# Weighted and plain neighbour sums: rows stored in source order and gathered in destination order, one-hots and rows in fp32

## The reference, cut to what matters

```python
# layer 3 (weighted): row = src, col = dst, deg = number of edges that leave a node (at least 1)
norm = edge_weights / jnp.sqrt(deg[row] * deg[col])
out  = segment_sum(x[row] * norm[:, None], col, num_segments=N)
# layer 4 (plain): edges and self loops, deg of both
norm = deg_inv_sqrt[row] * deg_inv_sqrt[col]
out  = segment_sum(label_mat[row] * norm[:, None], col, num_segments=num_nodes)
```

## Time and profile before

| | us |
|---|---|
| median of 3 runs (19801.2 to 19824.42) | 19813.48 |
| span of the profiled execution, first to last instruction | 17009.2 |
| `spread1`, from 14870 to 15608 | 738 |
| `tally1`, from 15608 to 15910 | 302 |
| `spread0`, from 16005 to 16606 | 601 |
| `tally2`, from 16606 to 16916 | 310 |
| `edge_keys`, up to its last gather | 2271 |

### The profile page before, as it was taken

How to read it: one execution, slowest core, us unless ns; L and a number is a source line. 1 busy time by engine, 2 the same in 40 slices (tenths; PEclk the granted TensorE clock), 3 DMA queues, 4 the chain that set the end, 5 groups by cost and what they waited for, 6 DMA issues and landing times. The chain is left out here.

```text
span 17009.2 us, 405783 instructions
## 1 busy us (share of the span) xinstructions
PE 9949.2 (58%) x119882; PEld 7747.5 (46%) x119882; DVE 11124.4 (65%) x27289; ACT 5234.6 (31%) x15775; POOL 9202.6 (54%) x10645
## 2 busy tenths in 40 slices
PE   2000047777777647974896599569926666433454
PEld 1000024444444237864785488458824444333324
DVE  6830046777776767985897599759954555466757
ACT  0000012222222014651564266236613333221120
POOL 7777777777777104431442244124427777585270
PEclk9755555555555569987997899699958777756656
DMA  3833357677678437645663666276612222134445
GB/s 117 327 93 102 102 87 80 85 85 85 85 86 79 80 102 209 176 126 150 186 176 91 196 176 176 56 227 176 175 48 61 65 65 65 45 129 143 148 152 161
DMA packets 2548685, 2116.02 MB, mean 124 GB/s; under 512 B 418374, under 2 KB 2314590, under 8 KB 2541593
## 3 DMA queue, kind: packets, MB, share of 16 engines
q1 hardware_dynamic: 2225086, 1439.58, 31.2%
q0 software_dynamic: 309216, 539.46, 19.4%
q10 hardware_dynamic: 14216, 135.01, 2.3%
HBM read 1290.57 MB, written 726.03 MB: 119 GB/s over the span
## 5 line engine op out<-in xcount | busy, mean ns | idle before, releaser
L627 POOL DMA_INDIRECT attend_rows<-key_rows,attend_fetch_now x1824 | 1747.7, 958 | 2056.5 <-PE attend_seg L1670 1729.3
L1714 ACT ACTIVATE attend_hot<-attend_lane_hot,attend_share 128x128 f32<-128x128 fp8e4 x7296 | 2228.5, 388 | 1209.9 <-DVE attend_share L1737 976.5
L627 POOL DMA_INDIRECT edges_rows<-raw,edges_perm_now x1824 | 2007.5, 1101 | 629.1 <-issue 602.4
L627 POOL DMA_INDIRECT keys_rows<-table,keys_staged x1564 | 1658.6, 1060 | 471.0 <-issue 471.0
L1670 PE MATMUL attend_seg<-attend_rows,attend_hot 128*128 128x49 f32 x14592 | 1816.8, 278 | 122.9 <-ACT parts_layer L1718 85.7
L1670 PEld LDWEIGHTS attend_seg<-attend_rows,attend_hot 128*128 128x128 f32 x14592 | 1734.3, 195 | 207.1 <-issue 201.9
L627 POOL DMA_INDIRECT mlp_xin<-table,mlp_staged x1564 | 1511.3, 966 | 472.7 <-issue 469.3
L1044 PE MATMUL edges_ps_t<-ident,edges_attr 128*40 128x128 f32 x1824 | 425.4, 413 | 1861.6 <-ACT edges_attr L1099 1833.9
L633 POOL DMA_INDIRECT messages<-spread_out,spread_place_now x912 | 1027.9, 1127 | 385.9 <-issue 276.5
L1657 PE MATMUL attend_qx<-attend_table,attend_oht 128*128 128x90 bf16 x21888 | 1087.8, 207 | 124.8 <-DMA attend_oht<-src_hots 113.0
L1481 POOL COPY expand_table<-k 128x156 bf16 x912 | 289.3, 317 | 1602.4 <-issue 947.3
(11 more groups left out here) (517 smaller groups left out, 23761.4 us busy)
## 6 DMA issues: line engine op xcount, KB each, us to landing
key_rows<-expand_out SPq DMA_DIRECT2D x304, 624.0 KB
attend_ea<-edge_attrs SPq DMA_DIRECT2D x912, 160.0 KB
tally_rows<-messages SPq DMA_DIRECT2D x152, 864.0 KB, 4.8
attend_table<-q SPq DMA_DIRECT2D x1832, 67.5 KB
expand_oht<-dst_hots SPq DMA_DIRECT2D x304, 384.0 KB, 4.8
attend_oht<-src_hots SPq DMA_DIRECT2D x912, 128.0 KB
attend_lane_hot<-src_hots_by_edge SPq DMA_DIRECT2D x912, 128.0 KB
raw<-keys_rows ACTq DMA_DIRECT2D x46, 2176.0 KB
```

The lines of the kernel that those rows point to most:

```text
L627: return nc.gpsimd.indirect_dma_start(out=out, out_offset=None, in_=table, in_offset=bass.IndirectOffsetOnAxis(ap=index, axis=0))
L1714: ins = nc.scalar.activation(hot[p][:, u, c, :], lane_hot8[r][:, u, c, :], ACT.Copy, scale=share[p][:, u, c:c + 1])
```

## The change

`spread` now serves both layers. VectorE writes fp32 rows straight from PSUM to `out` (a product with the weights, or a copy), with no split, and GpSimd stores the chunk as it is, in source order, with one plain DMA of 576 KB to `k.rows_a` ("rows_by_source"). `tally` gathers in place of loading: six indirect DMAs of 128 rows of 768 bytes per chunk, from the places in `k.origin`, into a ring of four. The one-hots are fp32, and TensorE does 24 fp32 matmuls a chunk in place of 72 bf16 ones. The zeroing of `k.msg` is gone; one row of each partition of `k.rows_a` is zero, for granules that no source has. `k.origin` is the inverse of `k.place`, and is built in `edge_keys` after the sort, with the same steps as `k.place`.

```diff
@@ edge_keys, SyncE
-            with sp.Fori(0, ZEROS) as n:
-                sp.dma_start(k.msg.rearrange("(p u) w -> p (u w)", p=P)[:, bass.ds(n * ZW, ZW)], zeros[...]).then_inc(s_out, 16)
+            sp.dma_start(k.rows_a.rearrange("(p r) w -> p r w", p=P)[:, NS, :], zeros[:, 0:GR * F]).then_inc(s_out, 16)
@@ edge_keys, VectorE, behind the sort
+            for q in range(4):
+                dve.wait_ge(s_mm, 13 + q)
...
+                for half in (slice(0, P // 2), slice(P // 2, P)):
+                    ch.done(v.tensor_tensor(under, rows_of(level[0:UT, :], P // 2), bc(k.iota[0:UT, half], KB), ALU.is_le))
+                    ch.done(v.tensor_tensor(under, under, rows_of(jump[0:UT, :], P // 2), ALU.mult))
+                    ch.done(v.tensor_reduce(at[0:UT, q, half], under, AX, ALU.add))
...
+            ch.done(v.tensor_tensor(k.origin[:], k.origin[:], part, ALU.add))
@@ spread, GpSimd
-                for u in range(EX):
-                    scatter(nc, k.msg, place_now[:, r, u:u + 1], out[r][:, u, :], NS * P - 1).then_inc(s_scat[r], 16)
+                pool.wait_ge(s_ev, (n + 1) * EX)
+                pool.dma_start(k.rows_a.rearrange("(p r) w -> p r w", p=P)[:, bass.ds(n * EX, EX), :], out[r][:]).then_inc(s_kept[r], 16)
@@ spread, VectorE
-                split(v, ch, msg[:], [by3[r][:, :, j, :] for j in range(3)], rest[:])
+                    if weighted:
+                        ins = v.tensor_tensor(out[r][:, u, :]..., got..., bc(k.w_a[:, ...], F), ALU.mult)
+                    else:
+                        ins = v.tensor_copy(out[r][:, u, :], got)
@@ tally, GpSimd (new) and SyncE (gone)
-                sp.dma_start(rows[b][:], k.msg.rearrange("(u p) w -> p u w", p=P)[:, bass.ds(n * EX, EX), :]).then_inc(s_load[b], 16)
+                pool.wait_ge(s_now, n + 1)
+                after(pool, s_seg, n - RINGS + 1)
+                for u in range(EX):
+                    gather(nc, rows[r][:, u, :], k.rows_a, origin_now[:, r, u:u + 1]).then_inc(s_rows[r], 16)
@@ tally, TensorE and VectorE
-        hot = [ph.sb(f"hot{b}", [P, EX * GR, P], BF16) for b in two]
+        hot = [ph.sb(f"hot{b}", [P, EX * GR, P]) for b in two]
-                        for j in range(3):
-                            ins = nc.tensor.matmul(ps[b][...], hot[b][:, u * GR + c, :], rows[b][:, u, at:at + F], ...)
+                        ins = nc.tensor.matmul(ps[b][...], hot[b][:, u * GR + c, :], rows[r][:, u, c * F:(c + 1) * F], ...)
+                    listed(n + 2, (r + 2) % RINGS)      # VectorE: 6 places per lane for the gathers two chunks on
```

More of the change, by code:

```diff
@@ L64 @@
 EX = 6
[L65 to L68, removed]
 KDOT = F + 2
@@ L423, in _ @@
             ins.then_inc(s_perm, 1)
+            pe.wait_ge(s_inv, 1)
+            t.transpose(small[0:NT, 128:128 + NT], base[0][0:NT, 0:NT], k.ident[0:NT, 0:NT]).then_inc(s_mm, 1)
+            for q in range(4):
+                pe.wait_ge(s_inv, 2 + q)
+                t.matmul(small[0:UT, 256:256 + KB], ended[0:NT, q * UT:(q + 1) * UT], base[1][0:NT, :], start=True, stop=True)
+                t.matmul(small[0:UT, 320:320 + KB], ended[0:NT, q * UT:(q + 1) * UT], steps[0:NT, :], start=True, stop=True).then_inc(s_mm, 1)
+            pe.wait_ge(s_inv, 6)
+            for q in range(4):
+                ins = t.transpose(wide[:, q * UT:(q + 1) * UT], at[0:UT, q, :], k.ident[0:UT, 0:UT])
+            ins.then_inc(s_mm, 1)
         @block.vector
@@ L2337, in _, with spread @@
             v.tensor_copy(k.tail[:, 0:F], sums[1][:, C - 1, :]).then_inc(s_step, 1)
-def spread(nc, k):
+def spread(nc, k, weighted):
     CHN, RINGS = NS // EX, 4
     with ExitStack() as ctx:
-        ph = Phase(nc, ctx, "spread1")
-        two = range(2)
+        ph = Phase(nc, ctx, "spread1" if weighted else "spread0")
+        two, ring = range(2), range(RINGS)
         oht = [ph.sb(f"oht{b}", [P, EX, W // 2], BF16) for b in two]
@@ L2420, in _ @@
             v = nc.vector
-            ch = Chain(dve, s_step)
-            by3 = [out[r][:].rearrange("p u (c j f) -> p (u c) j f", c=GR, j=3) for r in ring]
             def step(n, r, t):
+                after(dve, s_kept[r], t * 16)
                 for u in range(EX):
                     dve.wait_ge(s_exp, n * EX + u + 1)
[L2427 to L2431, removed]
-                split(v, ch, msg[:], [by3[r][:, :, j, :] for j in range(3)], rest[:])
-                dve.sem_inc(s_msg, 1)
@@ L2435, in _ @@
[L2435 to L2438, removed]
[L2439 to L2446 removed]
+                    got = ps[u][:, 0:GR * F]
+                    if weighted:
+                        ins = v.tensor_tensor(out[r][:, u, :].rearrange("p (c f) -> p c f", f=F), got.rearrange("p (c f) -> p c f", f=F),
+                                              bc(k.w_a[:, bass.ds((n * EX + u) * GR, GR)], F), ALU.mult)
+                    else:
+                        ins = v.tensor_copy(out[r][:, u, :], got)
@@ L2467, in steps @@
                 step(r, r, 0)
-            with eng.Fori(1, CHN // RINGS) as t:
+            with eng.Fori(1, LOOPS - 1) as t:
                 for r in ring:
                     step(t * RINGS + r, r, t)
+            for r in ring:
+                step((LOOPS - 1) * RINGS + r, r, LOOPS - 1)
         block = ph.block()
@@ L2543, in tally @@
[L2543 to L2575 removed]
+                pe.wait_ge(s_rows[r], (t + 1) * (16 * EX))
```

175 lines of the change are left out of this document (57 added, 118 removed).

## The result

The changed kernel took 19916.59 us (median of 4, 19895.34 to 19974.88) against 19807.34 (median of 4, 19799.03 to 19824.42) of the kernel before: ratio 1.0059, interval 1.0041 to 1.0076, +109 us. Timed again later it was 1.0113 (1.0096 to 1.0129), +223 us. Forecast were +262 us and 20075. The direction was right, and 19916.59 lies inside the stated range, 7 us above its lower end; the size was off by more than half in the first timing and by 15% in the second.

A forecast was written before the change was run, and what follows sets the result against it. It took GpSimd's queue of scatters to bound both spreads, and VectorE's `tally_hot` to fill the tallies' chunks. +50 (weighted layer), +179 (plain layer) and +33 (`edge_keys`) gave +262 us: 19813.5 becomes 20075, range 19910 to 20280.

The forecast's parts named there:

- The part outside the span: Whole launch: 2804 us of the 19813.5 lie outside the profile's 17009.2 us span and stay unchanged.
- the sign that would tell: Whole launch: a time change much unlike the span's change would mean the 2804 us outside the span moved.
- The spreads: Both spread phases: ScalarE's six table copies, 0.64 us apart, set 4.2 us a chunk, 337 us each.
- Rival 2: Spreads: the plain store costs GpSimd 7.7 us a chunk, each spread 266 us longer, 20607 us; chance 0.07.
- The removed scatters: Spreads: taking out six scatters a chunk and the split's passes gives -401 us in `spread1`, -264 in `spread0`.
- The tallies: Both tally phases: six gathers and a hold make 9.8 us a chunk, 753 us each, +451 and +443.
- The hold: Tallies: VectorE's one-hots with two SBUF operands delay one GpSimd gather, 2.35 us lost a chunk.
- The term of TensorE: Tallies: 24 fp32 matmuls take 2.5 us a chunk at the higher clock, 5.0 at the lower, under GpSimd's 7.45.
- Rival 1: Tallies: the one-hots don't hold the gathers; 574 us a tally, -134 us in all, 19680 us; chance 0.10.
- `edge_keys`: Phase `edge_keys`: new VectorE passes stretch gathers, +38 us, zeroing gone, -5 us; together +33 us.
- The rest as unchanged: Everything outside the four spread and tally phases and `edge_keys`, `expand` included: no change, 0 us.
- the four terms of the layers: Spread and tally of each layer: -401 and +451 in the weighted one, -264 and +443 in the plain one.

The follow-up runs named there:

- e_psiota: Changed kernel with iota copied to PSUM, where the tally's one-hots read it; ratio 1.0079 to the kernel before, tallies 799 us.
- a_pad32: Changed kernel plus an unused SBUF tile of 32 bytes a partition; 20230.67 us, ratio 1.0109 to the kernel before.
- e_pad64: Kernel before plus an unused SBUF tile of 64 bytes a partition; 19969.26 us, ratio 0.9974 to the kernel before.
- b0_again: Kernel before, unaltered, profiled a second time; 19859.93 us, ratio 0.999.
- a0_again: Changed kernel, unaltered, profiled and timed again; 19572.75 us, ratio 1.0113 to the kernel before.
- b0_third: Kernel before, unaltered, profiled a third time; 19335.08 us, span 19333.4 us.
- e_parts: Changed kernel with rows stored as three bf16 parts, 72 bf16 matmuls a chunk and iota in PSUM; ratio 1.0112 to the kernel before, tallies 737 us.

## Why the prediction came out as it did

- *The part outside the span, counted as unchanged.* Wrong. There is no such part. The profile shown was of a shorter execution, and its `spread0` (601 us) was not the one that is timed (789 to 802). The prediction itself named the sign that would tell, and it came: a span that moved by 2925 us where the time moved by 109. The step from a 17009 us span to a 19813 us time was taken on trust.
- *The spreads.* The mechanism was right: ScalarE's six copies set the pace, the plain store is hidden. The spacing was too short, 0.72 us between copies in the steady state and not 0.64, and 0.6 more at the turn of a chunk: 5.0 us a chunk, not 4.2, 42 us a layer. Rival 2 (a store of 7.7 us) is false: 0.53.
- *The removed scatters.* Mis-sized through the profile: -408 in the plain layer where -264 was forecast, because the slow issue beside the scatters went with them; -360 where -401 was forecast in the weighted one, and the 42 of the spread above are the whole of it, since the phase before took its 738 us again.
- *The tallies.* The hold was right in kind and nearly in size: one gather a chunk of 3.67 us, 10.2 us a chunk where 9.8 were forecast. The term of TensorE was mis-sized by a factor of two. "Eight of the same width take 0.99 us" were eight records of four matmuls, so 24 matmuls are 5.0 us at the higher clock and 10.25 at the lower, where 2.5 and 5.0 were taken. It happened to equal the other bound, so by luck the total looked nearly right (802 us where 753 were forecast: 76 x 0.45 = 34 of it are the chunk, and 15 the 23 us beside the chunks where 8 were taken) for a reason that was half missing. Rival 1 would have been wrong too: `e_psiota` took the hold away and gained 3 us.
- *Page "SBUF — State Buffer", section "Who interferes with whom", of the Trainium skill.* A gather held for 3.67 us by fp32 one-hots agrees with its rule on two SBUF operands, and `e_psiota` with the other side of it: with one operand in PSUM the gather takes 0.94. Its inference that `tensor_tensor` does not stall descriptor generation is contradicted again.
- *`edge_keys`.* Right: +36 and +31 measured, +33 forecast.
- *"The rest as unchanged".* This term, put at nothing, is the step that failed for the first timing. The new tile `k.origin` moved every later tile by 1824 bytes, and the stores of `expand` gained 78 us. By the table the four terms of the layers were off by +41, -144, +47 and +57, which leaves +1: errors larger than the total's, of both signs, that cancelled by luck. Without the gain of `expand` the change cost 261 us (`a_pad32` against `e_pad64`), 1 us from the forecast, for the same reason.
- *What stays open.* In the first timing the four phases differ by +214 us (2482.8 against 2268.8 of `b0_again`), `edge_keys` by +31, `expand` by -79, together +166, and +109 was measured. Of the 153 us between forecast and measurement 79 are `expand`, 17 the other terms, and 57 stay open. `edges`, which the change does not touch, was 4388 us in that profile and 4493 in `b0_again`, 4127 in `a0_again` and 4077 in `b0_third`. That scatter is larger than what is missing. What makes an execution issue slowly, or why one was free of it, no run here shows.

## What to carry to other kernels

Hold the span against the time before any row is used: the sixteen later profiles agree with their times to 2 us, and the one that did not was of an execution unlike the timed ones. Count a matmul's records, not its lines, before TensorE is called free, and take away two bounds together when each alone gives nothing. A new SBUF tile moves all that are allocated behind it, so ask which DMA-bound phase gets a new start address, and align what it stores to 128 bytes, as both fast starts here were.

## What the runs showed of the hardware

- A phase bound by its DMA traffic, loads and stores of 832-byte rows out of SBUF, moved 299 GB/s when the stored tile started at a multiple of 64 bytes (128 in both builds), and 280 from 32 bytes past one.
- While GpSimd issued indirect DMAs, TensorE, VectorE and ScalarE went 3 to 4 us without an instruction together (`spread0`), and TensorE took bf16 matmuls with 0.5 us gaps (`e_parts`, 786 us of issue in two tallies). It cost `spread0` about 200 us (598 against 789 and 802). The shown profile, with the same scatters, had none. Direct loads beside the same 72 matmuls (the tallies before, 302 us) and a plain store from GpSimd (the spreads after) did not bring it on.
- An fp32 matmul with 128 columns of weights is two records of 0.21 us at the clock 0.50, and the weight loads are as long as the matmuls (778.98 and 779.32 us of an 804 us tally); the bf16 loads of `e_parts` are 0.113 us each. The *Trainium skill*, page "TensorE: Matmul & The Clock Gate", section "Weight-path perf modes — Fast Weight Load (FWL) and DoubleRow", says that the fast load is on for 128 weights and any type but fp32; the rows agree. It would account for a good part of what fp32 one-hots, as the stationary side, cost TensorE: 779 us a tally, where the three bf16 products took 303 in `e_parts` (granted clock 0.56) and 185 to 195 in the kernel before (0.73 to 0.77).
- TensorE, busy without a gap through a tally of 802 us in the changed kernel, was granted 0.50 the whole time; the tallies before, busy 62 to 64%, had 0.73 to 0.77.
